# Rounding x in a PSUM bank that the attention also uses, with every engine's order rewritten

## Time and profile before

| | us |
|---|---|
| median of 3 runs | 535.02 |
| lowest, highest run | 531.51, 536.55 |
| the profiled execution's own time | 538.59 |
| its span (first to last instruction) | 536.8 |
| PE busy, weight loads apart | 447.4 (83%) |
| DVE busy | 414.8 (77%) |
| ACT busy | 364.9 (68%) |
| POOL busy | 376.2 (70%) |
| mean granted TensorE clock | 0.977 |
| in the chain that ended last: PE | 44% |
| in that chain: DMA `ahT<-ah_stack` | 23% |

### The profile page before, as it was taken

The page is one execution under the profiler, slowest core; times in us unless marked ns, Lnnn a source line. Parts: engine busy times, 40 slices in busy tenths (PEclk is TensorE's granted clock), DMA queues, the critical chain, the costliest instruction groups (busy, mean ns, idle before and its releaser), DMA issues.

```text
span 536.8 us, 21323 instructions
## 1 busy us (share of the span) xinstructions
PE 447.4 (83%) x8612; PEld 309.0 (58%) x8612; DVE 414.8 (77%) x776; ACT 364.9 (68%) x559; POOL 376.2 (70%) x854
## 2 busy tenths in 40 slices
PE   0138887998998889999998899899999998999975
PEld 0025554665665556666666466566666666667653
DVE  3897988886886777888887688868888887876572
ACT  3544988785775676777776677667777777777640
POOL 3864468875777756778878767757788878766262
PEclk9999999998998898999999899989999999999998
DMA  8202127553464753466656666735566654565443
GB/s 296 80 11 60 40 61 146 98 94 66 113 113 78 118 99 74 107 114 118 117 96 101 116 117 116 113 73 107 108 115 117 108 98 79 107 109 100 107 72 90
DMA packets 175010, 54.40 MB, mean 101 GB/s; under 512 B 164224, under 2 KB 174272, under 8 KB 174912
## 3 DMA queue, kind: packets, MB, share of 16 engines
q1 hardware_dynamic: 174480, 52.90, 51.9%
q10 hardware_dynamic: 432, 0.13, 0.1%
HBM read 7.54 MB, written 4.19 MB: 22 GB/s over the span
## 4 chain that ended last, share of the span: by engine, by line
PE 44%; DMA 23%; DVE 10%; POOL 8%; issue 6%; ACT 3%; SPq 2%; DVEq 0%; POOLq 0%
DMA ahT<-ah_stack 23%; PE up L372 12%; PE gt L560 10%; PE bank_b L584 7%; PE gt L574 5%; POOL y L1575 3%; POOL ah_stack L1569 3%; PE scores L517 3%; DVE y L928 2%; PE bank_b L378 2%; ACT ffn_gate L1335 2%; PE gt L372 1%; PE scores L541 1%; PE bank_q L372 1%; SPq L1859 1%
## 5 line engine op out<-in xcount | busy, mean ns | idle before, releaser
L1322 ACT ACTIVATE probs<-scores 128x768 f32<-128x768 f32 (+1 forms) x101 | 80.3, 795 | 57.0 <-PE scores L541 51.3
L584 PE MATMUL bank_b<-probs,vals 64*32 64x64 f32 (+1 forms) x3904 | 74.8, 220 | 13.8 <-DVE vals L905 13.7
L584 PEld LDWEIGHTS bank_b<-probs,vals 64*32 64x32 f32 (+1 forms) x3904 | 60.6, 108 | 31.2 <-DVE vals L905 16.9
L372 PE MATMUL up<-wgu_hi,xT 128*128 128x352 f16 x248 | 66.0, 334 | 0.0
L372 PE MATMUL gt<-wgu_hi,xT 128*128 128x352 f16 x256 | 62.4, 312 | 1.2 <-DVE y L928 1.2
L372 PE MATMUL bank_q<-wproj_hi,xT 128*128 128x512 f16 x128 | 45.2, 394 | 16.9 <-DMA xT<-x_stack 9.8
L787 DVE SCALAR_TENSOR_TENSOR up<-up,h_gain,gate 128x704 f32<-128x704 f32 x31 | 29.7, 958 | 30.6 <-PE up L372 29.2
L1575 POOL TENSOR_TENSOR y<-y,x_all 128x256 f32<-128x256 f32 x31 | 23.1, 746 | 40.5 <-DVE y L928 40.5
L560 PE MATMUL gt<-wdn_lo,ahT 128*128 128x256 f16 x192 | 46.4, 277 | 0.0
L574 PE MATMUL gt<-wo_hi,ahT 128*128 128x256 f16 x120 | 26.6, 288 | 21.7 <-DMA ahT<-ah_stack 21.6
L1556 POOL TENSOR_TENSOR ah_stack<-h_grid,h_coarse 128x704 f16<-128x704 bf16 x31 | 42.5, 1370 | 2.5 <-DVE h_grid L824 2.5
(11 more groups left out here) (231 smaller groups left out, 1370.2 us busy)
## 6 DMA issues: line engine op xcount, KB each, us to landing
out<-y SPq DMA_DIRECT2D x32, 128.0 KB, 3.3
x_all<-x SPq DMA_DIRECT2D x20, 128.0 KB, 3.9
x_all<-x SPq DMA_DIRECT2D x3, 512.0 KB, 4.4
x_all<-wproj SPq DMA_DIRECT2D x1, 768.0 KB, 7.4
dn_raw<-wd SPq DMA_DIRECT2D x1, 704.0 KB, 9.1
probs<-wg SPq DMA_DIRECT2D x1, 640.0 KB, 5.6
probs<-wu SPq DMA_DIRECT2D x1, 640.0 KB, 8.0
xT<-x_stack SPq DMA_TRANSPOSE x34, 4.0
```

Of the source, the lines that this page charges most:

```text
L372: done = e.matmul(out, lhs[i][:, kt, :], rhs[j][:, kt, lo:hi], start=n == 0, stop=n == len(terms) - 1)
L584: done = e.matmul(pv_bank(i)[32 * n:32 * n + 32, grp * P + q:grp * P + q + HB], va, pr, start=first and grp == 0, stop=last and grp == 3)
L1322: e.activation(probs[j % P_BUFS][:, grp, :, window(j)].rearrange("p (b e) w -> p b e w", b=2), score_banks(j, grp)[:, :, :, window(j)], AC ...
```

## The change

The FP4 rounding of x for tiles 4 and up moves from the two SBUF buffers `xq` into the first half of `bank_b`. `norm_x(t)` writes there, `square_x` reads it there, `up_x` and `grid_x` work on it there. Its turn in the bank is between `attend(t-4)` and `v_mm(t)`: `norm_x(t)` now waits for `attend(t-4)` and for `grid_x(t-1)` (there is one buffer instead of two), and `v_mm(t)` waits for `grid_x(t)` instead of `attend(t-4)`. The arithmetic and the number of instructions are the same. `norm_x` keeps its two inputs in SBUF; `up_x` and `grid_x` now have one input in SBUF and one in PSUM.

The lists of PE, DVE, ACT, POOL and SP are all rewritten. In a pass of the loop:

- PE: `wo_mm(t-4)` comes one group of scores later. The rest is as before (`qk_mm` moves over the loop's boundary only).
- DVE: `attend(t-3)` comes before `gated(t-4)`; `norm_x(t+1)` right behind `gated`; `squares`, `up_x`, `grid_x` of tile t+1 before `grid_h(t-2)` and `values(t+1)`; `unit` at the end; `lo_qk(t)` before `hidden(t-2)`.
- ACT: `hi_q`, `hi_k`, `hi_xn` before the third `exp` instead of behind it.
- POOL: `lo_att(t-3)` comes before `add_x(t-4)`; the eleven steps of `root(t+1)` run without other work between them; `hi_h`, `lo_h` of tile t-2 end the pass.
- SP: `store(t-5)` and `refill(t-7)` come before `ah_transpose(t-3)`.

The lists of the first and last tiles are rewritten as well. The diff, cut to its core:

```diff
@@ -114,7 +114,13 @@
         xn = [x_ring[:, i] for i in range(XN_BUFS)]
-        xq = [x_ring[:, XN_BUFS + i] for i in range(2)]
+
+        def in_psum(t):
+            return 4 <= t
+
+        def x_round(t):
+            return bank_b[:, 0:D] if in_psum(t) else x_ring[:, XN_BUFS + t % 2]
+
...
@@ -454,8 +460,8 @@
             def v_mm(t):
                 e.wait_ge(*xT_landed(t))
                 e.wait_ge(s_lo_wproj, KT)
-                if t >= 4:
-                    e.wait_ge(s_att, t - 3)
+                if in_psum(t):
+                    e.wait_ge(s_x_step[GRID], t + 1)
                 elif t == WD_TURN + 1:
                     e.wait_ge(s_lo_wd, len(WD_GROUPS))
                 elif t >= 1:
...
             scores(2, 3)
-            qk_mm(4)
             for t in range(4, 31):
+                qk_mm(t)
                 gate_mm(t - 2)
                 scores(t - 1, 0)
                 v_mm(t)
                 scores(t - 1, 1)
                 pv(t - 3)
+                scores(t - 1, 2)
                 wo_mm(t - 4)
-                scores(t - 1, 2)
                 up_mm(t - 2)
                 up_mm_last(t - 2)
                 pv_rest(t - 3)
...
-                qk_mm(t + 1)
+            qk_mm(TILES - 1)
+            scores(TILES - 2, 0)
...
+            pv(TILES - 2)
             up_mm(TILES - 1)
+            gate_mm(TILES - 1)
             up_mm_last(TILES - 1)
-            pv(TILES - 2)
             pv_rest(TILES - 2)
-            gate_mm(TILES - 1)
+            pv(TILES - 1)
             back(TILES - 2)
-            pv(TILES - 1)
-            wo_mm(TILES - 3)
             pv_rest(TILES - 1)
             back(TILES - 1)
             down_mm(TILES - 3, 0, 4)
...
@@ -762,21 +772,23 @@
 
             def norm_x(t):
                 e.wait_ge(s_x_step[RSCALE], t + 1)
-                if t >= 2:
-                    e.wait_ge(s_x_step[GRID], t - 1)
-                e.tensor_tensor(blocks(xq[t % 2]), blocks(xn[t % XN_BUFS]), per_block(x_rscale[:]), ALU.mult
+                if in_psum(t):
+                    e.wait_ge(s_att, t - 3)
+                if t >= 1:
+                    e.wait_ge(s_x_step[GRID], t)
+                e.tensor_tensor(blocks(x_round(t)), blocks(xn[t % XN_BUFS]), per_block(x_rscale[:]), ALU.mult
                                 ).then_inc(s_x_step[NORM], 1)
 
             def up_x(t):
                 e.wait_ge(s_x_step[SQUARE], t + 1)
-                e.scalar_tensor_tensor(xq[t % 2], x_square[:], SQ_BASE, xq[t % 2], ALU.add, ALU.add).then_inc(s_x_step[UP], 1)
+                e.scalar_tensor_tensor(x_round(t), x_square[:], SQ_BASE, x_round(t), ALU.add, ALU.add).then_inc(s_x_step[UP], 1)
 
             def grid_x(t):
                 e.wait_ge(s_x_step[UP], t + 1)
                 if t >= 1:
                     e.wait_ge(s_lo_qx, t)
                     e.wait_ge(s_hi_qx, t)
-                e.scalar_tensor_tensor(x_grid[:], x_square[:], SQ_BASE, xq[t % 2], ALU.add, ALU.subtract
+                e.scalar_tensor_tensor(x_grid[:], x_square[:], SQ_BASE, x_round(t), ALU.add, ALU.subtract
                                        ).then_inc(s_x_step[GRID], 1)
 
             def hidden(t):
...
             for t in range(4, 31):
-                unit(t)
-                norm_x(t + 1)
+                if exists(t + 4):
+                    ln_stats(t + 4)
+                wide_x(t + 1)
+                rscale_x(t + 1)
+                lo_qk(t)
                 hidden(t - 2)
                 amax_h(t - 2)
                 wide_h(t - 2)
-                lo_qk(t)
                 rscale_h(t - 2)
                 denom(t - 3)
                 norm_h(t - 2)
+                attend(t - 3)
                 gated(t - 4)
-                attend(t - 3)
+                norm_x(t + 1)
                 up_h(t - 2)
+                squares(t + 1)
+                up_x(t + 1)
                 if exists(t + 4):
                     ln_moments(t + 4)
-                squares(t + 1)
-                if exists(t + 2):
-                    amax_x(t + 2)
+                grid_x(t + 1)
                 grid_h(t - 2)
                 values(t + 1)
                 if exists(t + 2):
-                    wide_x(t + 2)
-                if exists(t + 2):
-                    rscale_x(t + 2)
-                if exists(t + 5):
-                    ln_stats(t + 5)
-                up_x(t + 1)
-                grid_x(t + 1)
+                    amax_x(t + 2)
+                unit(t + 1)
...
             up_h(TILES - 1)
             grid_h(TILES - 1)
+            hi_h_last()
             gated(TILES - 3)
-            hi_h_last()
             gated(TILES - 2)
             gated(TILES - 1)
             add_last()
...
@@ -1188,7 +1199,7 @@
                 e.wait_ge(s_x_step[NORM], t + 1)
                 if t >= 1:
                     e.wait_ge(s_x_step[GRID], t)
-                e.activation(x_square[:], xq[t % 2], ACT.Square, scale=math.sqrt(SQ_GAIN)).then_inc(s_x_step[SQUARE], 1)
+                e.activation(x_square[:], x_round(t), ACT.Square, scale=math.sqrt(SQ_GAIN)).then_inc(s_x_step[SQUARE], 1)
...
             for t in range(4, 31):
                 square_x(t)
                 silu(t - 2)
                 exp(t - 1, 0)
                 exp(t - 1, 1)
-                exp(t - 1, 2)
                 hi_q(t)
                 hi_k(t)
                 if exists(t + 2):
                     hi_xn(t + 2)
+                exp(t - 1, 2)
                 keep_pv(t - 3)
                 exp(t - 1, 3)
                 down_silu(t - 4)
                 square_h(t - 2)
                 hi_att(t - 3)
                 square(t + 1)
+            square_x(TILES - 1)
...
-            pad_vals()
             ln_parts(0)
             ln_parts(1)
+            pad_stack(0)
             root(-1, SEED)
             root(-1, Y_SQ)
             root(-1, ARG)
-            pad_stack(0)
             root(-1, LINEAR)
             root(-1, QUAD)
             root(-1, CUBIC)
             root(-1, STEP)
             root(-1, Z_SQ)
             root(-1, Z_ARG)
-            norm_w(1)
             root(-1, LAST_FACTOR)
             root(-1, ROOT)
+            x_norm(0)
             pad_stack(1)
-            x_norm(0)
+            x_norm(1)
+            norm_w(1)
+            lo_xn(0)
+            norm_w(3)
+            norm_w(5)
+            pad_vals()
             steps(0)
-            x_norm(1)
-            lo_xn(0)
+            ln_parts(2)
+            lo_xn(1)
+            coarse_x(0)
             ones(0)
-            coarse_x(0)
-            norm_w(3)
             fine_x(0)
             round_w(1)
-            ln_parts(2)
-            norm_w(5)
-            ones(1)
             floor_ss(0)
-            lo_xn(1)
+            x_norm(2)
             round_w(3)
-            x_norm(2)
+            lo_qx(0)
+            hi_qx(0)
             ln_parts(3)
...
             for t in range(4, 31):
-                root(t, CUBIC)
-                root(t, STEP)
-                fine_x(t)
-                root(t, Z_SQ)
-                root(t, Z_ARG)
-                root(t, LAST_FACTOR)
-                root(t, ROOT)
-                if exists(t + 2):
-                    x_norm(t + 2)
-                lo_h(t - 3)
+                coarse_h(t - 2)
                 hi_qx(t)
-                hi_h(t - 3)
-                if exists(t + 3):
-                    ln_parts(t + 3)
                 if exists(t + 2):
                     lo_xn(t + 2)
-                coarse_h(t - 2)
-                lo_qx(t)
+                fine_h(t - 2)
+                coarse_x(t + 1)
+                lo_att(t - 3)
                 add_x(t - 4)
-                lo_att(t - 3)
                 floor_ss(t + 1)
                 root(t + 1, SEED)
                 root(t + 1, Y_SQ)
                 root(t + 1, ARG)
-                coarse_x(t + 1)
-                fine_h(t - 2)
                 root(t + 1, LINEAR)
                 root(t + 1, QUAD)
+                root(t + 1, CUBIC)
+                root(t + 1, STEP)
+                root(t + 1, Z_SQ)
+                root(t + 1, Z_ARG)
+                root(t + 1, LAST_FACTOR)
+                root(t + 1, ROOT)
+                fine_x(t + 1)
+                if exists(t + 3):
+                    x_norm(t + 3)
+                lo_qx(t + 1)
+                hi_h(t - 2)
+                if exists(t + 4):
+                    ln_parts(t + 4)
+                lo_h(t - 2)
...
             for t in range(8, 31):
-                stack_transpose(t + 1)
-                ah_transpose(t - 2)
-                if exists(t - 8) and exists(t - 8 + X_RING):
-                    refill(t - 8)
+                x_transpose(t + 1)
+                stack_transpose(t)
                 store(t - 5)
-                x_transpose(t + 3)
+                if exists(t - 7) and exists(t - 7 + X_RING):
+                    refill(t - 7)
+                ah_transpose(t - 3)
             store(TILES - 6)
```

(95 more changed lines are left out.)

305 lines of the change are left out of this document (153 added, 152 removed).

## The result

The changed kernel takes **519.64 us** (median of 4 runs, 517.02 to 520.53) against 533.69 for the kernel before in the same session (531.51 to 536.55): a ratio of 0.973, 95% interval 0.966 to 0.979. It is faster than before, 5.6 us slower than the 514 forecast and inside the range. The profiled execution took 519.24 (before: 538.6), so the sum of the steps, -23.7, stands against a measured -19.4.

What follows compares the result with a forecast made beforehand. No engine is full; a chain of waits through the ahT DMA closes the pass, and irregular passes lose 19.5 us. Terms -15.5, -4.2, -2 and -2 from 538.6 give 514.9, taken as 514; range 503 to 535.

Steps and rivals of the forecast that it cites:

- The path to v_mm: In an ordinary pass, v_mm waits for grid_x and starts 0.3 us late, at 7.87, making the pass 13.88 us.
- norm_x in the bank: On DVE, norm_x writing to PSUM takes 0.41 us instead of a median 1.54, falling into a gap of POOL's work.
- its 1.1 us buy nothing: The 1.1 us of DVE time won per pass gain nothing by themselves, as DVE is busy 11.75 of 14.05.
- The slack: Ahead of wo_mm on PE, ahT lands 0.65 us before it is wanted, where there was a wait of 0.39.
- If no idle stretch is long enough for the clock to fall, 15.5 are won: Of 19.5 us lost in irregular passes, 15.5 are won if PE's idle stretches stay too short for the clock to fall.
- the 4 forecast: Seven late DMAs of about 1.0 to 1.6 us extra, less 0.65 each, leave some 4 us of waits.
- The clock rival: PE's short idle stretches still let the clock fall, so only 4.2 us and the ends are won: 530 us; chance 0.18.
- The ends: Before and after the loop: start -2 us (between -6 and +4), end -2 us (between -3 and 0).
- The slower rival: norm_x stands until POOL's lo_att and add_x are over, slipping about 1.9 us per pass: 559 us or more; chance 0.10.
- passes -9.6 for -4.2: The 26 ordinary passes of the loop fall from 14.04 to 13.88 us each, giving 4.2 us.
- irregular passes: Loop passes slowed by late ahT DMAs and clock falls lose 19.5 us over 26 passes; 15.5 were to be won.

Runs made afterwards that it cites:

- e2: The kernel before with lo_att ahead of add_x on GpSimd and attend ahead of gated on VectorE, nothing else: 531.8 us, ratio 0.994.
- e1: The changed kernel's orders on every engine, but x rounded in two SBUF buffers as before instead of the bank: 511.7 us, ratio 0.959.
- e3: The changed kernel with 128 empty instructions ahead of TensorE's first one: 515.5 us, ratio 0.963.
- e6: The changed kernel with norm_x one place later, behind up_h, once with the bank and once with SBUF: 522.7 and 514.0 us.
- e4: The changed kernel with wo_mm moved behind up_mm and up_mm_last in the pass: 508.6 us, ratio 0.952.
- e11: e1 with values ahead of grid_h on VectorE and the v product ahead of the first score group, behind gate_mm, on TensorE: 525.5 us.
- e12: e11 with, behind the pass, hi_q(31) and hi_k(31) ahead of down_silu(27), lo_qk(31) first, stack_transpose(31) ahead of ah_transpose(28): 530.1 us.
- e10: e1 with wo_mm behind up_mm_last, SyncE's two last transposes exchanged, the v product right behind qk_mm, values ahead of grid_h: 535.5 us.

## Why the prediction was right, and where it was wrong

**The path to v_mm: right, 0.07 too long.** From `pv_rest` (305.74) on, `gated` came at 4.65 and `norm_x` at 5.05, as worked out; `up_h` at 5.38, as worked out. `squares` came at 6.18, not 6.44: I had counted `ln_moments` behind `up_h` although it moved, and taken off only 0.1 for it later. The v product started at 7.80 for 7.87 and waited 0.15 for 0.3. From `pv` to the next `pv_rest` it is 4.13 for 4.24. From the v product to `pv` it is 1.74 for 1.77. Hence 13.67 for **13.88**: 0.07, 0.03 and 0.11 too long, worth 5.4 us over 26 passes.

**norm_x in the bank: right in size (0.42 for 0.41), and right that its 1.1 us buy nothing** (e2). What stood beside it on GpSimd decided, not its target (e1). The 0.19 a pass (the prediction's estimate) by which the Trainium skill's rule on PSUM sources ("VectorE: DVE Perf Modes", its section on the TRN2 errata) would have made the path longer is not there: medians of 0.423, 0.418 and 0.420 in the bank stand against 0.415, 0.456 and 0.425 in SBUF (e1). The 0.456 of `up_x` is again a meeting (it ends 0.28 behind `add_x`); in the kernel before it took 0.402. The 0.19 also counted `norm_x`, which reads SBUF, as one of three; with the two that read PSUM it would be 0.13, an estimate by the same figures. And the rows of `up_h` and `grid_x` differ in width and in source at once, so they alone could not show that there is no extra start cost; e1 shows it.

**The slack: right in sign and nearly in size** (0.54 for 0.65). It was added up from three parts, two of the order and one of the later `v_mm`, and e1 bears that out: without the bank 0.30 is left, so some 0.24 of the slack are bought by the bank's 0.21 a longer pass.

**"If no idle stretch is long enough for the clock to fall, 15.5 are won": the step that failed.** 9.0 were won. The prediction took the late landings over from the trace before, 1.0 to 1.6 us longer. Five came 1.6 to 2.5 longer and left waits of 1.02, 1.10, 1.13, 1.68 and 1.91 us, 6.8 in all, for the 4 forecast. Behind three of them the granted clock fell to 0.50 for 3.4 us, at 1.7 us each, 5.1 in all; behind 1.02 and 1.13 it did not, behind 1.10 it did. 6.8 and 5.1, less the 0.7 of the short pass, are about the 11.1. The clock rival, given 0.18, was thus half true. Putting `store` and `refill` first hardly changed the number of late landings (six over 5 us in the passes before, five after): what the five met was TensorE's instruction transfers (e3).

**The ends.** The start gave -1.4 for -2, with `root(0)` at 0.18 to 0.20 a step as expected; what took the rest back was not tried. The end gave +0.6 for -2. `scores(31)` waits 1.3 for a transpose issued at 479.84, which I had not followed; but neither of the two orders tried there won more than 0.8, so what holds the end is open.

**The slower rival** (0.10, 559 us) needed `norm_x` to meet `lo_att`. It does not in the changed kernel (310.79 against 311.33). Its price was wrong too: in e6 `norm_x` waited for the end of `lo_att` only, and `add_x`, which had not started, waited for `norm_x`. By the fixed 0.28 behind the other's end, a meeting with the whole of `lo_att` would cost at most 0.67 + 0.28 - 0.42 = 0.53 us (an estimate), not the 1.9 forecast and too little for 559 us.

The terms: passes -9.6 for -4.2, irregular passes -9.0 for -15.5, start -1.4 for -2, end +0.6 for -2. Two errors of 5 and 6 us nearly cancelled, which was luck: the 514 was better than its steps.

## What to carry to other kernels

Take a change of order and a change of place apart before crediting either: here the order gave all of the gain and the place took 0.2 us a pass from it. Where `norm_x` (two SBUF inputs) met an instruction of GpSimd, the later of the two paid the whole overlap but for some 0.14 us, and the one that started first paid nothing (e6). When a transfer is late now and then, what matters is the slack ahead of its reader, not its median: a step that shortens the ordinary pass by 3% but leaves no slack (e2) gave 0.6%, and one that leaves the pass as it is and adds slack until no landing is late for it (e4) gave 2%. Before moving an instruction off the chain of waits, follow the second chain too; in a tight loop it is a few tenths behind.

## What was not expected of the hardware

- The transfers that bring TensorE's own instructions (16 KB, every 258 instructions, about two a pass) are moved beside the data: of the transposes of 4.1 us in which one began 1.5 to 4.1 us after the issue, 67 of 99 took 5.2 to 6.7. 128 empty instructions at the start of the program change which passes are slow.
- How long TensorE stood idle does not by itself tell whether the granted clock falls. e11 and e12 have the same order in the passes, and in every pass a wait of 1.23 us for `grid_h`:

```profile
PE up L523 <- DVE h_grid L834: 32.0, 26, 1.3
```

(the same line in both). In e12 the clock fell five times in the passes, twice with no other wait of the pass near; in e11 not once between 86 and 457 us. In e10, with 1.00 us and 0.31 us of idle time in a pass, it fell five times. What decides was not found.
